# Channel attention in a four-layer network: halo rows carried from band to band in place of being projected again

## The reference

```
x_pad = pad(x, 3 on each side)
q    = einsum('bchw,oc->bohw', x,     w_q)
kmap = einsum('bchw,oc->bohw', x_pad, w_k)
vmap = einsum('bchw,oc->bohw', x_pad, w_v)
kwin, vwin = 7x7 windows of kmap, vmap
kwin = concat([kwin[:, :half] + rel_h, kwin[:, half:] + rel_w])
attn = softmax(q * kwin over the 49 places)
out  = sum(attn * vwin over the 49 places)
```

## Time and profile before

| | us |
|---|---|
| median of three runs | 8120.62 (8116.14 to 8125.58) |
| the profiled execution, as timed | 8114.73 |
| its span in the profile | 8113.0 |
| TensorE clock granted, mean | 0.982 of full speed |
| channel attention, from its first load of weights to its last tile, about | 3222 to 7455 |

### The profile page before, as it was taken

One profiled execution on the slowest core, in us unless ns is written; L12 is line 12 of the kernel. 1 busy time (PEld: TensorE's weight loads), 2 busy tenths in 40 slices (PEclk: granted clock), 3 DMA queues, 4 the chain that ended last, 5 costly groups with the idle time before them and its releaser, 6 DMA issues. The chain is left out here.

```text
span 8113.0 us, 142887 instructions
## 1 busy us (share of the span) xinstructions
PE 7639.8 (94%) x55554; PEld 6564.9 (81%) x55554; DVE 5850.9 (72%) x9141; ACT 3633.4 (45%) x7024; POOL 4558.3 (56%) x1996
## 2 busy tenths in 40 slices
PE   5999998899998997899999999999999999997999
PEld 4777776789997775688888888888888888886999
DVE  5666665344443554999898988999898988996664
ACT  3556565333332332445555454545555455544222
POOL 3555551033331000578778787878877787876232
PEclk9999999999998998999999999999999999998999
DMA  3111114855558773000000000000000000002452
GB/s 143 57 67 58 59 60 154 279 142 144 144 148 232 206 198 92 8 19 9 16 19 13 11 14 19 15 18 11 13 19 14 11 13 19 16 9 74 149 162 81
DMA packets 616222, 595.11 MB, mean 73 GB/s; under 512 B 464085, under 2 KB 481621, under 8 KB 610374
## 3 DMA queue, kind: packets, MB, share of 16 engines
q1 hardware_dynamic: 581318, 483.44, 21.3%
q0 software_dynamic: 33856, 96.69, 3.3%
q10 hardware_dynamic: 576, 8.39, 0.3%
HBM read 394.64 MB, written 193.76 MB: 73 GB/s over the span
## 5 line engine op out<-in xcount | busy, mean ns | idle before, releaser
L1826 POOL TENSOR_TENSOR e_ev<-e_se,e_v 128x2048 f32<-128x2048 f32 (+1 forms) x896 | 3308.9, 3714 | 898.5 <-ACT e_se L1789 893.5
L1789 ACT ACTIVATE e_se<-e_stage 128x512 f32<-128x512 f32 x3136 | 1869.7, 598 | 2041.6 <-PE e_stage L1656 1996.2
L1913 DVE SCALAR_TENSOR_TENSOR e_stage<-e_k,e_rl,e_qp 128x512 f32<-128x512 f32 x3136 | 2307.8, 747 | 301.4 <-ACT e_se L1789 262.8
L1663 PE MATMUL e_pe_sum<-e_ident,e_se 128*128 128x128 f32 x12544 | 1877.0, 272 | 12.4 <-ACT e_se L1789 12.2
L1663 PE MATMUL e_pv_sum<-e_ident,e_ev 128*128 128x128 f32 x12544 | 1869.4, 272 | 0.4 <-POOL e_ev L1826 0.4
L1663 PEld LDWEIGHTS e_pe_sum<-e_ident,e_se 128*128 128x128 f32 x12544 | 1555.7, 140 | 240.9 <-ACT e_se L1789 16.8
L1663 PEld LDWEIGHTS e_pv_sum<-e_ident,e_ev 128*128 128x128 f32 x12544 | 1483.9, 141 | 226.9 <-issue 174.5
L1656 PE MATMUL e_stage<-e_top,e_minus 128*128 128x512 f32 x3136 | 1507.2, 481 | 51.2 <-DVE e_stage L1913 46.6
L911 POOL DMA_DIRECT2D agg<-c_ot x384 | 334.8, 874 | 878.5 <-ACT c_ot L989 768.9
L403 POOL TENSOR_TENSOR a_pr<-a_pr,a_rden 128x480 f32<-128x480 f32 x512 | 495.0, 988 | 543.9 <-DVE a_rden L636 543.9
L1656 PEld LDWEIGHTS e_stage<-e_top,e_minus 128*128 128x128 f32 x3136 | 595.0, 190 | 111.0 <-DVE e_stage L1913 81.1
(11 more groups left out here) (170 smaller groups left out, 11454.2 us busy)
## 6 DMA issues: line engine op xcount, KB each, us to landing
qkv<-b_ot SPq DMA_DIRECT2D x120, 512.0 KB, 5.9
c_xt<-qkv SPq DMA_DIRECT2D x384, 160.0 KB, 3.8
agg<-c_ot POOLq DMA_DIRECT2D x384, 160.0 KB, 2.5
f_ws<-in_L_w_sets SPq DMA_DIRECT2D x32, 1152.0 KB, 8.0
a_xb<-in_x SPq DMA_DIRECT2D x24, 768.0 KB, 5.1
a_xr<-in_x SPq DMA_DIRECT2D x32, 512.0 KB, 3.8
x<-a_xr SPq DMA_DIRECT2D x32, 512.0 KB, 2.7
b_xc<-x SPq DMA_DIRECT2D x32, 512.0 KB, 6.1
```

The lines of the kernel that those rows point to most:

```text
L1663: last = nc.tensor.matmul(acc[:, c * PART:(c + 1) * PART], lhsT=src[:, c * PART:(c + 1) * PART], rhs=ident[:], is_transpose=True, start=j ...
L1789: nc.scalar.activation(se[(t * K2 + o) % NSE][:, i], stage[:, bank_of(t, j), :], ACT.Exp)\
L1826: nc.gpsimd.tensor_tensor(split(ev[(t * NG2 + g) % NEV][:, 0:size]), split(se[(t * K2 + o) % NSE][:, i:i + size]), window(v[h], h, u, o, i ...
L1913: nc.vector.scalar_tensor_tensor(rows(stage[:, bank_of(t, j), :]), win, rl[:, h, o:o + 1], rows(qp[:]), ALU.add, ALU.mult).then_inc(multip ...
```

## The change

Two neighbouring bands of an image share six rows of halo. Before, each band projects all its 22 rows with the padding columns. Now it projects only what is new and real:
- Keys and values of 16 fresh rows, 64 columns each, in two chunks of 8 rows (`K1`, `K2`, `V1`, `V2`, 512 columns). The first band of an image opens it, and also projects the three rows ahead of these (`K0`, `V0`, 192 columns). Padding stays zero from a clear at the start.
- The last six rows of the buffers of the band before are copied to their first six, by transfers within SBUF that ACT issues: `carry_keys` at tap 1 and `carry_values` at tap 18 of an even tile, one each for a half; `carry_near` at tap 3 of tile 0 and `carry_pairs` at tap 3 of tile 1, for the extremes, which both halves of a band share in one buffer. Where an image opens, these transfers bring zeros.
- DVE makes extremes of fresh rows only: two pair steps and six reductions for each chunk, three, three and two rows at a time, at taps 11 to 30 (before: 4 to 33). For the first half the padding columns of `pair` have a small step of their own ahead of each pair step (L1931, 48 elements).
- The values' chunks are at taps 6 and 12 of the odd tile (and 2 for `V0`), the queries' at 24 and 29 of the even one, the keys' at 7 and 14 (and 0 for `K0`).
- POOL clears `k`, `v`, `near` and `pair` too, and SP's first load waits for all of it.

Each carry stands between two exponentials, where there was none before. The core of the diff:

```diff
-        PROJ_AT = ({0: 0, 7: 1, 14: 2, 24: 3, 30: 4, 33: 5}, {0: 6, 2: 7, 4: 8, 6: 9})
+        HALO = K2 - 1
+        NH2 = NB * HALVES
+        FRESH, WAS = HALO, R2
+        PROJ_AT = ({0: "K0", 7: "K1", 14: "K2", 24: "Q1", 29: "Q2"}, {2: "V0", 6: "V1", 12: "V2"})
+        ROWS_OF = {"0": (PAD, PAD), "1": (FRESH, RT), "2": (FRESH + RT, RT)}
...
+        KEYS_AT, VALUES_AT, NEAR_AT = 1, 18, 3
+        PIECES = ((0, 3), (3, 3), (6, 2))
+        NEAR_FIRST = [(4, "K0", 0, 0), (6, "K0", 1, 0), (8, "K0", 0, 1), (10, "K0", 1, 1)]
+        NEAR = [(11, "K1", 0, 0), (13, "K1", 1, 0), (14, "K1", 0, 1), (15, "K1", 0, 2), (16, "K1", 0, 3), (17, "K1", 1, 1),
...
+        def opens(H):
+            return H // HALVES % RB == 0
+        def parts(H):
+            return [p for p in ("K0", "K1", "K2", "Q1", "Q2", "V0", "V1", "V2") if opens(H) or p not in ("K0", "V0")]
...
-            def project(n, h, c, g, t=None):
-                w, first, size = PROJ[c]
+            def project(H, p, g, t=None):
+                c = parts(H).index(p)
                 if g == 0:
...
+                    if H or c:
+                        pe.wait_ge(proj_copied, made(H, p) - 1)
+                    if c and parts(H)[c - 1][0] == "K":
+                        pe.wait_ge(near_step, nears(H, parts(H)[c - 1]))
...
+                    rhs = fresh(xb[:, g], p)
+                last = nc.tensor.matmul(packed(pj, p), lhsT=wt[:, "QKV".index(p[0]), g, (H % 2) * PART:(H % 2 + 1) * PART], rhs=rhs,
                                         start=g == 0, stop=g == HALVES - 1)
                 if g == HALVES - 1:
                     last.then_inc(projected, 1)
...
+            def carry_keys(H):
+                act.wait_ge(multiplied, (2 * H - 2) * NTAP)
+                to = k[H % 2]
+                if opens(H):
+                    act.dma_start(to[:, 0:PAD * PW], zeros[:, 0:PAD * PW]).then_inc(keys_carried, 16)
                 else:
-                    to, src = (q, k, v)[w][h % 2][:, first:first + size], pj[:, 0:size]
+                    act.dma_start(to[:, 0:HALO * PW], to[:, WAS * PW:(WAS + HALO) * PW]).then_inc(keys_carried, 16)
+            def carry_values(H):
+                act.wait_ge(weighted, (2 * H - 2) * NG2)
+                to = v[H % 2]
+                if opens(H):
+                    act.dma_start(to[:, 0:PAD * PW], zeros[:, 0:PAD * PW]).then_inc(values_carried, 16)
+                else:
+                    act.dma_start(to[:, 0:HALO * PW], to[:, WAS * PW:(WAS + HALO) * PW]).then_inc(values_carried, 16)
+            def carry_near(H):
+                act.wait_ge(ext_step, exts(H - 2, NEXT_))
+                if opens(H):
+                    act.dma_start(near[:, :, 0:PAD * PW], zeros.rearrange("p (i n) -> p i n", i=2)).then_inc(near_carried, 16)
+                else:
+                    act.dma_start(near[:, :, 0:HALO * PW], near[:, :, WAS * PW:(WAS + HALO) * PW]).then_inc(near_carried, 16)
+            def carry_pairs(H):
+                act.wait_ge(near_step, nears(H - 1))
+                size = (HALO - 1) * PW
+                if opens(H):
+                    act.dma_start(pair[:, :, 0:2 * PW], zeros[:, 0:4 * PW].rearrange("p (i n) -> p i n", i=2)).then_inc(near_carried, 16)
+                else:
+                    act.dma_start(pair[:, :, 0:size], pair[:, :, WAS * PW:WAS * PW + size]).then_inc(near_carried, 16)
+            def copy_projection(H, p):
+                if H >= 2 and p == "V1" and not opens(H) or H >= 2 and p == "V0":
+                    act.wait_ge(weighted, (2 * H - 2) * NG2)
+                if H >= 2 and p == "K2":
+                    act.wait_ge(keys_carried, carries(H))
+                if H >= 2 and p == "V2":
+                    act.wait_ge(values_carried, carries(H))
+                act.wait_ge(projected, made(H, p))
+                if p[0] == "Q":
+                    a = (int(p[1]) - 1) * TPX
+                    to, src = q[H % 2][:, a:a + TPX], pj[:]
+                else:
+                    to, src = fresh((k if p[0] == "K" else v)[H % 2][:], p), packed(pj, p)
                 nc.scalar.activation(to, src, ACT.Copy).then_inc(proj_copied, 1)
...
-                if j - HALVES in PROJ_AT[u] and not (final and t // 2 == HALVES - 1):
-                    copy_projection(n, t // 2 + 1, PROJ_AT[u][j - HALVES])
+                H = n * HALVES + t // 2 + 1
+                if 2 <= H < NH2 and u == 0:
+                    if j == KEYS_AT:
+                        carry_keys(H)
+                    if j == VALUES_AT:
+                        carry_values(H)
+                if j == NEAR_AT and H % 2 == 1 and H + 1 + u < NH2:
+                    (carry_near, carry_pairs)[u](H + 1 + u)
+                p = PROJ_AT[u].get(j - HALVES)
+                if H < NH2 and p in parts(H):
+                    copy_projection(H, p)
...
+            act.wait_ge(cleared, CLEARED["e"])
             normalise(0)
...
-            nc.gpsimd.memset(xb[:], 0.0).then_inc(cleared, 1)
+            for x in (xb, *k, *v, near, pair):
+                nc.gpsimd.memset(x[:], 0.0).then_inc(cleared, 1)
...
+            def near_step_of(H, s):
...
+                if s == 0 and H:
+                    dve.wait_ge(ext_step, exts(H, 0))
+                    dve.wait_ge(near_carried, carries(H + 1))
+                if s == 0 and H >= 2 and h == 1:
+                    dve.wait_ge(keys_carried, carries(H))
...
+                    if h == 0:
+                        a = pair[:, i, first * PW:first * PW + 1]
+                        z = k[0][:, first * PW + 1:first * PW + 2]
+                        edge = [[PW, size], [WW + 2, 2], [1, PAD]]
+                        nc.vector.tensor_scalar(bass.AP(tensor=a.tensor, offset=a.offset, ap=[a.ap[0]] + edge),
+                                                bass.AP(tensor=z.tensor, offset=z.offset, ap=[z.ap[0]] + edge), 0.0, None, op)\
+                            .then_inc(near_step, 1)
+                        dve.wait_ge(near_step, nears(H) + near_before(H, s) + 1)
+                        to, z = to[:, first:first + size, PAD:PAD + WW], grid(k[0][:])[:, first:first + size, PAD + 1:PAD + 1 + WW]
                     else:
-                        to, a, z = to[:, 0:HR - 1, :], a[:, 0:HR - 1, :], z[:, 1:HR, :]
-                    nc.vector.tensor_tensor(to, a, z, op).then_inc(near_step, 1)
+                        to, z = (grid(t)[:, first - 1:first - 1 + size, PAD:PAD + WW] for t in (pair[:, i], k[1][:]))
+                    nc.vector.tensor_tensor(to, packed(pj, p), z, op).then_inc(near_step, 1)
                     return
...
+                low, part = (0, size) if p == "K0" else PIECES[piece - 1]
+                away = (1, PW)[h]
+                at = (first + low) * PW if h == 0 else (first + low - HALO) * PW + PAD
...
+                                ap=[a.ap[0], [PW, part], [1, WW], [3 * away, 2], [2 * away, 2]])
+                nc.vector.tensor_reduce(grid(near[:, i])[:, first + low:first + low + part, PAD:PAD + WW], pairs, AX.XY, op)\
+                    .then_inc(near_step, 1)
```

More of the change, by code:

```diff
@@ L1413, in channel_attention @@
         v = [sb(f"v{u}", [PART, HPX]) for u in range(2)]
-        pair = [sb(f"pair{i}", [PART, HPX]) for i in range(2)]
-        near = [sb(f"near{i}", [PART, HPX]) for i in range(2)]
+        pair = sb("pair", [PART, 2, HPX])
+        near = sb("near", [PART, 2, HPX])
         high = sb("high", [PART, BPX])
@@ L1492, in tiles, with made, near_of, nears @@
             return n * (TPB * per) + (t * per + more)
-        def halves(n, h, per, more):
-            return n * (HALVES * per) + (h * per + more)
+        def opens(H):
+            return H // HALVES % RB == 0
+        def parts(H):
+            return [p for p in ("K0", "K1", "K2", "Q1", "Q2", "V0", "V1", "V2") if opens(H) or p not in ("K0", "V0")]
+        def made(H, p=None):
+            return sum(len(parts(i)) for i in range(H)) + (parts(H).index(p) + 1 if p else 0)
+        def near_of(H):
+            return [x for x in NEAR_FIRST if x[3] == 0 or H % HALVES == 0] + NEAR if opens(H) else NEAR
+        def nears(H, p=None):
+            last = [x[1:] for x in near_of(H)].index((p, 1, 0)) + 1 if p else 0
+            return sum(near_before(i, len(near_of(i))) for i in range(H)) + near_before(H, last)
+        def near_before(H, s):
+            return sum(2 if x[3] == 0 and H % HALVES == 0 else 1 for x in near_of(H)[:s])
+        def exts(H, more):
+            return H * NEXT_ + more
+        def carries(H):
+            return 16 * (min(H, NH2 - 1) - 1)
         def window(t, h, u, o, i, taps):
@@ L1605, in _ @@
                 if n + 1 < NB:
-                    sp.wait_ge(projected, halves(n, 2, NPJ, 0))
+                    sp.wait_ge(projected, made((n + 1) * HALVES))
                     load_band(n + 1)
@@ L1709, in step @@
                     sum_weighted(n, t, 0, first=first)
+                H = n * HALVES + t // 2 + 1
                 for g in range(HALVES):
```

(38 more changed lines are left out.)

131 lines of the change are left out of this document (50 added, 81 removed), and 3 rows, old and new, of the table NEAR.

## The result

The changed kernel takes 8091.03 us (median of 7 runs, 8087.21 to 8100.14) against 8117.95 us for the kernel before on the same chip (8113.80 to 8125.58): ratio 0.9968, 95% interval 0.9957 to 0.9979. It is faster by 27 us, 0.3%, where 176 us were forecast. The sign was right, the size was not, and the time lies 106 us above the range's upper end.

A forecast was written before the change was run, and what follows sets the result against it. PE, near 97% busy, was taken as the bound, with DVE close. 100.2 + 83.4 + 0 - 7.7 = 175.9 us off 8114.73 gave 7938.8, or 7945 us with the median's offset; range 7890 to 7985.

The forecast's parts named there:

- edge steps: Tile 2: four small new 48-element steps on DVE, 0.2 us each plus 0.1 of lost overlap.
- value waits: Odd tiles: PE's waits for ACT's copy of values out of the single bank pj go, 83.4 us gained.
- PE after losing the early projections: Channel attention taps: no new neighbour on pj closer than four taps, so no new wait was priced.
- near rows "wanted at tap 11": Transfer of extremes issued at tap 3 is wanted at tap 11, some nine us later: cost 0.
- start of the stage: Six more arrays cleared before SP's first load, 10.7 us, less 3 us from a shorter chain: 7.7 us dearer.
- DVE's excess in even tiles: Tile 0 0.4 us more, tile 2 0.6 less, opening halves give back 0.8 three times: about 0 in sum.
- Fewer columns: Key and value projections on PE: 109.4 us less, 9.2 back for openings, so 100.2 us gained.
- Strided reductions: Tile 0: a DVE reduction of 192 outputs stays slow, 1.41 us from start to start.
- Rival 1: Tile 0's strided reductions turn fast, 70 us more gained: 7875 us; chance 7%.
- Carries on ACT: ACT's issues of 90 transfers within SBUF cost 0 us, with 40 us as the upper bound.
- Rivals 3 and 4: ACT's issues show, 7985 to 8044 us, 9%; or each carry holds ACT so long that the kernel is slower, 3%.
- Load of the next band: SP's load comes about 4 us later in the tile but keeps more than 8 us of slack: cost 0.

The follow-up runs named there:

- edge_tt: Changed kernel with the edge steps as TENSOR_TENSORs of the two neighbours, both read from SBUF: 8099.51 us, ratio 0.9971 to the kernel before.
- edge_reduce: Changed kernel with the edge steps as TENSOR_REDUCEs over the two neighbours, same results: 7998.76 us, ratio 0.9853 to the kernel before.
- the two small ones: Kernel before plus small extra DVE instructions within SBUF in each band's third tile, as TENSOR_SCALAR or as TENSOR_REDUCE: 8220.50 and 8136.22 us.
- pool_split: Changed kernel with POOL's multiplication of three or four taps issued as multiplications of one tap each: 8119.04 us, ratio 0.9995 to the kernel before.
- before_v_spread: Kernel before with the four value chunks in odd tiles at steps 0, 4, 8, 12 instead of 0, 2, 4, 6: 8032.81 us, ratio 0.9888.
- cover_values: On edge_reduce, V1 and V2 at steps 1 and 7 of odd tiles, not 6 and 12, where no image opens: 7986.77 us.
- near_first: On edge_reduce, ACT issues the carry of extremes at step 0 of even tiles rather than step 3: 7983.62 us.
- no_carry: On edge_reduce, ACT's four carries per two halves and the waits for them left out: 7978.15 us.
- early_load: On edge_reduce, SP's first load waits for the clearing of its own buffer only, not all seven clearings: 7989.11 us.
- before_small_ts: Kernel before plus small extra DVE TENSOR_SCALARs (128x48, within SBUF) in each band's third tile: 8220.50 us, ratio 1.0116.

## Why the prediction was wrong, step by step

**The step that failed** is the price of the edge steps: "having a tenth of its elements they are nearer to the lower end, and I take 0.2, plus 0.1 of lost overlap". They took 1.45 in the mean, and the time was 92 us longer than with edges of 0.25. My upper bound of 0.59 was the start to start of a whole 512-element step; but that row reads an operand from PSUM. So it is with every TENSOR_SCALAR and TENSOR_TENSOR of the stage before: it reads from PSUM or writes there. This one, for instance, reads SBUF and writes PSUM, and takes 735 to 843 ns each time, though POOL is in the middle of an instruction at the start of all 124:

```profile
L1887 DVE TENSOR_SCALAR e_ext<-e_near,e_rl 128x512 f32<-128x512 f32 x124 | 93.0, 750 | 0.0
```

Only its reductions, reciprocals and statistics stay within SBUF, and those aren't held either, as the view of one buffer shows for the changed kernel (min/median/max ns):

```profile
L1999 DVE RECIPROCAL e_rs<-e_es x247: 939/946/954, 3375.5 to 7298.5; 128x128 f32<-128x128 f32 x124
```

So no row of this stage before had a TENSOR_SCALAR within SBUF beside POOL, and elements were the wrong measure. The Trainium skill, SBUF — State Buffer, section "Who interferes with whom", has the rule: VectorE and GpSimd share a port pair as an exclusive lock; tensor_scalar can enter a mode that takes it, an instruction with two SBUF inputs contends too, tensor_reduce never does on this chip. The holds in edge_tt, edge_reduce and the two small ones agree with all three (1461, 249, 1585 and 244 ns in the mean); the ports and the mode themselves no trace shows. Its "for the whole instruction" fits the changed kernel, where no edge is held past the end of the POOL instruction that it met; in pool_split it is too short for 15 edges, which were held over five or six. With POOL busy 80% of the time it should have been a rival; I had none that made an added DVE instruction dear by its form.

The sum against the runs:

| step of the prediction | forecast | measured | by |
|---|---|---|---|
| value waits | 83.4 off | 86 off (91 by the medians) | before_v_spread |
| edge steps | 0.3 us each, within DVE's sum | 92 us dearer than edges of 0.25: 79 held, 14 lower clock | after against edge_reduce |
| PE after losing the early projections | no new wait | 16 + 4 us | taps 2 and 5; 12.0 of it by cover_values |
| near rows "wanted at tap 11" | 0 | 15.1 us | near_first |
| start of the stage | 7.7 dearer | 9.2 | traces |
| DVE's excess in even tiles | about 0 | 19 to 25 us | lengths of stage and tiles |

From 7945: less 3 for the values, plus 92, 20, 15, 1.5 and 19 to 25, comes to 8090 to 8096; the median is 8091.0. That it closes so well is partly luck, since each term has an error of a few us, and the 7945 starts from a median of 8120.62 that four more runs brought to 8117.95. The edge steps alone don't make the prediction wrong: with them as reductions the kernel takes 7998.76, still 14 us above the range's upper end, and the other terms make that difference.

*Fewer columns.* Right: in odd tiles, where nothing of DVE binds, before_v_spread has 60.89 and the changed kernel 59.69. The difference, 1.20, with the 0.29 and 0.16 of new waits, is 1.65 us; 1032 products' columns fewer at 1.71 ns are 1.76.

*No new waits on PE* wasn't said of the sums, only of `pj`: "I see no new neighbour closer than four taps". True for `pj`, but taps 0 to 3 now had no projection unless a half opens an image, and PE's sum at tap 2 waits for ACT's copy of the last tile's sums: 0.29 us more in 55 tiles (16 us), as a tap of 1.40 us in place of 1.11 where nothing else is in it. Tap 5 has 0.16 more in 24 odd tiles (4 us).

*Strided reductions.* Right: 192 outputs of tile 0 came at 1.43 us from start to start (4864.86 to 4866.29 in the changed kernel's timeline), forecast 1.41. Rival 1 falls.

*Carries on ACT.* The issues were short, 0.47 and 0.64 us, and no wait of PE followed. Rivals 3 and 4 fall; no_carry leaves them at most 0.15 us per even tile. The landing was misjudged: "the near rows issued at tap 3 are wanted at tap 11" holds only where a half doesn't open an image. In an opening, K0's step waits for the transfer at tap 4. My text priced this wait at nothing.

*Excess of DVE in even tiles.* With the edges as reductions t0 is 0.6 and t2 0.9 us above the forecast, apart from tap 2. My sum let DVE begin at tap 11 with three banks of lead; it begins there with a wait of 1.9 us for ACT's copy of K1 and has no lead. Moving the keys up and spreading the steps took that back, but both moved together, so which of the two does how much stays open. The size of this term is the least certain: the stage lasts 4174.7 us from its first load of weights to its last tap, 4204.9 before, and what the other terms leave of that is 19 us; the even tiles' lengths against the forecast give up to 25. (For t2 the forecast's own terms give 62.95, not the 62.8 of the text.)

*Load of the next band, start of the stage.* The first cost nothing, as said. The second was 1.5 us dearer: the clears cost about what was said, but the chain behind them was hardly shorter, where 3 us were forecast (first tap 71.4 us after the first load of weights in early_load, 71.6 in the kernel before).

## What to carry to other kernels

Price an added instruction by its form and by who runs beside it, not by its elements: on DVE ask of each TENSOR_SCALAR and TENSOR_TENSOR where its operands lie, and if all are in SBUF and POOL is busy, let it last until POOL's instruction ends, and perhaps its run of them; a reduction over the two values, or an operand left in PSUM, avoids it. Add to a wait of PE of some 3 us what the next taps lose if the granted clock falls behind it. A projection or any other filler that you take away also takes the cover from a wait behind it; look at what is released one tap before it is wanted, and at the tiles of the profile before that have no filler. And read each "wanted at" on the exceptional iterations too, the openings and the first, with the waiting engine's lead taken off.

## What the runs showed of the hardware that I had not expected

A DVE TENSOR_SCALAR or TENSOR_TENSOR within SBUF, of 48 elements per partition, took 0.17 to 0.21 us with POOL idle and up to 4.05 us beside POOL's multiplications of 2048 (before_small_ts), up to 5.55 us beside a run of short ones of 512, and one of 18 elements there 6.8 us. A TENSOR_REDUCE of 48 outputs took 0.25 us, beside the long multiplications as with POOL idle. With shorter POOL instructions the kernel was slower, not faster. The profile books the hold as busy time of the DVE instruction: the sign is a duration far above its size, and an end together with POOL's.

Behind waits of PE of 3.3 us the granted clock of TensorE was 0.50 for 3.4 us or more in ten of fifteen cases of one kernel and stayed at 1.00 in five; where it fell, a tap of 1.57 us took up to 3.01.
